# The step-size product of a state-space block: weights stationary in four column tiles, tokens moving

## The reference, cut to what matters

```python
xn = (x - mu) * jax.lax.rsqrt(var + EPS) * ln_w + ln_b
zxbcdt = xn @ in_proj_w.T                       # 512 tokens, 256 features -> 1288
z, xBC, dt = jnp.split(zxbcdt, [D_INNER, D_INNER + CONV_DIM], axis=-1)   # dt: 8 heads
dt = jax.nn.softplus(dt + dt_bias)
A = -jnp.exp(A_log)
def step(h, inputs):
    dtk, xk, Bk, Ck = inputs
    decay = jnp.exp(dtk * A)
    h = h * decay[:, :, None, None] + dtk[:, :, None, None] * xk[..., None] * Bk[:, None, None, :]
    y = jnp.einsum('bhpn,bn->bhp', h, Ck)
    return (h, y)
```

## Time and profile before

| | us |
|---|---|
| median of 3 runs | 1272.43 |
| the runs | 1271.83, 1272.43, 1276.07 |
| the profiled execution | 1279.79 |
| its span in the trace | 1278.0 |
| PE busy in the span | 1155.5 (90%) |
| PEld busy | 804.7 (63%) |
| DVE busy | 996.8 (78%) |
| ACT busy | 779.9 (61%) |
| POOL busy | 636.8 (50%) |
| mean granted clock of PE | 0.962 of full |

### The profile page before, as it was taken

The page is one execution under the profiler, slowest core; times in us unless marked ns, Lnnn a source line. Parts: engine busy times, 40 slices in busy tenths (PEclk is TensorE's granted clock), DMA queues, the critical chain, the costliest instruction groups (busy, mean ns, idle before and its releaser), DMA issues. The chain is left out here.

```text
span 1278.0 us, 29867 instructions
## 1 busy us (share of the span) xinstructions
PE 1155.5 (90%) x10284; PEld 804.7 (63%) x10284; DVE 996.8 (78%) x2529; ACT 779.9 (61%) x1444; POOL 636.8 (50%) x554
## 2 busy tenths in 40 slices
PE   4687999999999999999999999999999999877387
PEld 2255666676667677666767667767776676655244
DVE  5765788788878887788888887888888887754486
ACT  1224676667776577667666766767566776766242
POOL 4572376327832584446643774178244653300375
PEclk9798999999999999999999999999899999988699
DMA  6042105310432024401540052203240133110511
GB/s 205 0 116 75 51 1 145 114 34 26 120 91 81 26 67 101 120 6 34 142 126 17 26 149 76 67 26 104 75 120 5 52 87 104 31 46 15 206 74 61
DMA packets 101524, 96.52 MB, mean 76 GB/s; under 512 B 17184, under 2 KB 76832, under 8 KB 100096
## 3 DMA queue, kind: packets, MB, share of 16 engines
q1 hardware_dynamic: 92912, 76.42, 20.0%
q0 software_dynamic: 6240, 17.57, 5.8%
q10 hardware_dynamic: 2224, 0.62, 0.2%
HBM read 71.49 MB, written 27.26 MB: 77 GB/s over the span
## 5 line engine op out<-in xcount | busy, mean ns | idle before, releaser
L891 ACT ACTIVATE T<-T,nmx 128x512 f32<-128x512 f32 x512 | 368.8, 724 | 229.0 <-DVE nmx L1257 227.0
L1257 DVE CUSTOM_DVE_ANT_0 T<-ps,am 128x512 f32<-128x512 f32 x512 | 346.2, 684 | 124.7 <-PE ps L680 123.1
L688 PE MATMUL pt<-ident,T 128*128 128x128 f32 x2048 | 329.1, 285 | 13.6 <-ACT PT L882 12.9
L688 PEld LDWEIGHTS pt<-ident,T 128*128 128x128 f32 x2048 | 234.4, 144 | 120.7 <-issue 88.9
L882 ACT COPY PT<-pt 128x512 f32<-128x512 f32 x352 | 202.0, 574 | 15.9 <-PE pt L688 15.2
L1373 POOL TENSOR_TENSOR dmask<-triu,dA 128x1024 fp32r<-128x1024 f32 x64 | 132.6, 2137 | 49.6 <-DVE dA L1101 49.5
L680 PE MATMUL ps<-k_st,q_st 64*128 64x512 f32 x512 | 132.0, 510 | 26.4 <-DMA q_st<-q_d 25.9
L705 PE MATMUL po<-PT,va 128*32 128x128 f32 x4096 | 140.0, 278 | 10.5 <-issue 6.2
L705 PEld LDWEIGHTS po<-PT,va 128*32 128x32 f32 x4096 | 105.9, 110 | 33.6 <-issue 32.3
L1411 POOL TENSOR_TENSOR rr<-se,nhalf 128x1 f32<-128x1 f32 x32 | 22.2, 694 | 210.1 <-DVE se L1187 199.5
L1348 POOL TENSOR_TENSOR xc<-xc,ygT 128x512 f32<-128x512 f32 x90 | 119.7, 1330 | 13.4
(11 more groups left out here) (212 smaller groups left out, 1970.7 us busy)
## 6 DMA issues: line engine op xcount, KB each, us to landing
k_st<-k_d SPq DMA_DIRECT2D x256, 64.0 KB, 2.2
q_st<-q_d SPq DMA_DIRECT2D x256, 64.0 KB, 2.4
am<-in_mask SPq DMA_DIRECT2D x8, 1024.0 KB, 5.5
k_d<-kp SPq DMA_DIRECT2D x32, 256.0 KB, 2.6
am<-in_adj POOLq DMA_DIRECT2D x8, 1024.0 KB, 10.8
q_d<-qp SPq DMA_DIRECT2D x128, 64.0 KB, 1.6
x_in<-in_x SPq DMA_DIRECT2D x8, 512.0 KB, 4.5
ctx_in<-in_ctxT SPq DMA_DIRECT2D x8, 512.0 KB, 4.2
```

Of the source, the lines that this page charges most:

```text
L688: ins = pe.transpose(pt[u % 2][:, kt * P:(kt + 1) * P], T[:, u % RING, kt * P:(kt + 1) * P], ident[:, :])
L891: act.activation(T[:, u % RING, :], T[:, u % RING, :], ACT.Exp, bias=nmx[:, u % RING:u % RING + 1], scale=-1.0).then_inc(sems["probs"], 1)
L1257: dve.tensor_tensor_reduce(T[:, u % RING, :], ps[(a * UNITS + u) % S_BANKS][:, :], ams[a % 2][:, qt, :], -1.0, 3e38, ALU.add, ALU.min, nmx ...
```

## The change

The product is turned round. The weights become the stationary operand, padded with zeros from 8 to 32 columns, and the tokens move, 128 at a time: chunk c goes to column tile c, and the result lies with its heads on partitions 32c to 32c + 7 and the chunk's 128 tokens along the columns. ACT copies this tile to a part of `th` that is free then, PE turns it by one 128x128 transpose into a second PSUM tile, and DVE adds the bias as before, reading 8 of each 32 columns. DVE zeroes the padding once at the start.

```diff
-    ("lnT",): {"pe": -1000, "act": -990}, ("dt1",): {"pe": -955, "act": -960, "dve": -935}, ("bc", 4): {"pe": -915, "act": -915},
+    ("lnT",): {"pe": -1000, "act": -990}, ("dt1",): {"pe": -965, "act": -950, "dve": -935}, ("dtT",): {"pe": -950, "act": -965}, ("bc", 4): {"pe": -915, "act": -915},
...
-                "lnT": [("lnT", 0), ("lnT", 1)], "dt1": [("dt",)], "bc": [_s], "cum": [("cum",)], "z": [_s],
+                "lnT": [("lnT", 0), ("lnT", 1)], "dt1": [("dtT",)], "dtT": [("dt",)], "bc": [_s], "cum": [("cum",)], "z": [_s],
...
-        wdt = sb("wdt", [P, KE, NH])
+        wdt = sb("wdt", [P, KE, P // C])
...
                     if k == "dt1":
-                        pe.wait_ge(read(("dt",), b), free_at(("dt",), b))
+                        if b == 0:
+                            pe.wait_ge(setup["pad"], 1)
+                        pe.wait_ge(read(("dtT",), b), free_at(("dtT",), b))
                         for kt in range(KE):
                             pe.wait_ge(read(("lnT", kt), b), read_at(("lnT", kt), b))
-                        for c in range(C):
-                            for kt in range(KE):
-                                ins = mm(bank(("dt",), b)[:, c * NH:(c + 1) * NH], xnT[:, kt, c * P:(c + 1) * P], wdt[:, kt, :], kt == 0, kt == KE - 1)
-                        ins.then_inc(full(("dt",), b), 1)
+                        for kt in range(KE):
+                            for c in range(C):
+                                ins = pe.matmul(bank(("dtT",), b)[P // C * c:P // C * (c + 1), 0:P], wdt[:, kt, :], xnT[:, kt, c * P:(c + 1) * P],
+                                                start=(kt == 0), stop=(kt == KE - 1), tile_position=(0, P // C * c), skip_group_check=True)
+                        ins.then_inc(full(("dtT",), b), 1)
+                    if k == "dtT":
+                        pe.wait_ge(read(("dt",), b), free_at(("dt",), b))
+                        pe.wait_ge(read(("dtT",), b), read_at(("dtT",), b))
+                        pe.transpose(bank(("dt",), b)[:, 0:P], th[:, 0, 0:P], ident[:, :]).then_inc(full(("dt",), b), 1)
...
+                    if k == "dtT":
+                        act.wait_ge(sems["silu"], at("silu", b, 0))
+                        act.wait_ge(full(("dtT",), b), full_at(("dtT",), b))
+                        act.copy(th[:, 0, 0:P], bank(("dtT",), b)[:, 0:P]).then_inc(read(("dtT",), b), 1)
...
+                dve.memset(wdt[:, :, NH:], 0.0).then_inc(setup["pad"], 1)
...
-                        dve.tensor_tensor(dts[:, 0, :, :], bank(("dt",), b)[:, 0:C * NH].rearrange("p (c h) -> p c h", h=NH), dtb[:, :, :], ALU.add).then_inc(read(("dt",), b), 1)
+                        dve.tensor_tensor(dts[:, 0, :, :], bank(("dt",), b)[:, 0:P].rearrange("p (c h) -> p c h", c=C)[:, :, 0:NH], dtb[:, :, :], ALU.add).then_inc(read(("dt",), b), 1)
```

More of the change, by code:

```diff
@@ L114 @@
     ("ln1",): {"dve": -1905, "pool": -1795}, ("ln2",): {"dve": -1895}, ("ln2r",): {"dve": -1840, "pool": -1685, "sp": -1505},
-    ("lnT",): {"pe": -1765, "act": -1920}, ("dt1",): {"pe": -1635, "act": -1881, "dve": -1738}, ("bc", 4): {"pe": -1685, "act": -1898},
+    ("lnT",): {"pe": -1765, "act": -1920}, ("dt1",): {"pe": -1635, "act": -1881, "dve": -1738}, ("dtT",): {"pe": -1630, "act": -1885}, ("bc", 4): {"pe": -1685, "act": -1898},
     ("conv", 4): {"pool": -1654}, ("bc", 5): {"pe": -1555, "act": -1878}, ("conv", 5): {"dve": -1674}, ("bc", 0): {"pe": -1465, "act": -1793},
@@ L301, in build @@
         m_read = [sem(f"m_read{k}") for k in range(M_BANKS)]
-        setup = {n: sem(f"setup_{n}") for n in ("act", "dve", "pool", "scaled")}
+        setup = {n: sem(f"setup_{n}") for n in ("act", "dve", "pool", "scaled", "pad")}
         PER = dict(
@@ L369, in build @@
                     ((cw[:, :, :], t["conv_w"].rearrange("(k p) j -> p k j", p=P)), consts), (column(cb, "conv_b"), consts)]
-        act_loads = [(column(lnw, "ln_w"), ln_in), (column(lnb, "ln_b"), ln_in), (matrix(wdt, "wdt"), w_in), (row(alog[:, :], "A_log"), consts)] + [
+        act_loads = [(column(lnw, "ln_w"), ln_in), (column(lnb, "ln_b"), ln_in), ((wdt[:, :, 0:NH], t["wdt"].rearrange("(k p) n -> p k n", p=P)), w_in), (row(alog[:, :], "A_log"), consts)] + [
             (row(dtb[:, c, :], "dt_bias"), consts) for c in range(C)] + [((triu[:, :], t["triu"]), consts), (matrix(wk, "wk"), kv_in), (matrix(wv, "wv"), kv_in)]
```

## The result

The changed kernel takes **1268.35 us** (1265.79 to 1271.05, 10 runs); the kernel before, measured beside it, 1274.14 (1270.13 to 1278.18, 10 runs). The ratio is 0.9946, 95% interval 0.9927 to 0.9966: faster by 0.5%, more than the 0.3% that can be told from no change. The profiled execution took 1269.45 us, its span is 1267.7, its mean granted clock 0.969 (before 0.962).

A forecast was written before the change was run, and what follows sets the result against it. PE was taken to set the pace on average (97% busy), with DVE close behind at the change. From the median, 1272.43 + 0.3 (delay) - 2.5 (batch 1) - 1.0 (clock) = 1269.2 us; range 1263.5 to 1275.5.

The forecast's parts named there:

- likeliest case: Whole kernel: DVE late next, gain from batch 1 and the clock; 1269.2 us, spanning 1265 to 1273, chance 0.45.
- The product, 1.70 to 0.54, and the transpose, 0.12: Step-size product on PE: column tiles cut it from 1.70 to 0.54 us, turning transpose adds 0.12; PE saves 1.04 a batch.
- rival 4: Product on PE: column tiles go one behind the other, scores 1.7 us late in six batches; about 1278 us, chance 0.03.
- The copy on ACT, 0.3 and hidden: ACT before the exponential: the 128x128 copy takes 0.3 us (0.2 to 0.4), hidden in 2.99 us of idle time.
- What is late next is DVE; nothing of 1.04 us reaches the end: Batches 2 to 7: later scores delay DVE, PE waits some 0.9 us for the gate; +0.05 us a batch, +0.3 for six.
- Rival 2: Batches 2 to 7: saved PE time counts in full, next scores 0.9 to 1.04 us earlier; near 1263.5 us, chance 0.17.
- rival 3: Scores behind the product: their delay is passed on through maximum and gate, up to +4.0 us; 1276.4 us, chance 0.12.
- Batch 1, -2.5: Batch 1: product moves into PE's wait for the query DMA and a clock fall goes; -2.5 us, between 0 and -3.3.
- The clock in batches 2 to 7, -6.2 for the profiled execution, -1.0 for the median: Behind the products: without 8-column matmuls no fall to half clock; -6.2 us profiled (bounds 0 and -6.2), -1.0 for the median.
- the other runs probably met few: Runs other than the profiled one: few clock falls, so the median counts one smaller fall less part of it, -1.0 us.
- Rival 1: Behind the products: the clock falls as before, with transposes and a new 0.9 us wait; 1271.9 us, chance 0.23.
- the rule on transposes: Between the score pairs: transposes don't count as PE activity, so falls continue; the sum loses -1.0 and batch 1's 1.7 us.

The follow-up runs named there:

- the padded kernels: Old product's moving operand zero-padded from 8 to 64 columns, against the kernel before: 1271.78 us, ratio 0.9964, at its old place; 1275.31 us, 0.9986, moved ahead of the scores.
- the two repeats: The changed kernel run again unaltered, against the kernel before: 1270.39 us, ratio 0.9963, and 1270.58 us, ratio 0.9949.

## Why the prediction was right, and where it was not

The forecast, 1269.2 in a range of 1263.5 to 1275.5, held the 1268.35 measured, and its likeliest case is the one that happened. That the time was met to 0.9 us is luck in part: the gain was 5.8 us where 3.2 were foretold, and the forecast started from a median 1.7 us under that of the ten runs. By its own steps:

- **The product, 1.70 to 0.54, and the transpose, 0.12.** Measured 0.57 and 0.11. The four column tiles run beside each other (their first four instructions start within 0.02 us); rival 4 falls.
- **The copy on ACT, 0.3 and hidden.** 0.27 us, in 2.22 us of idle time; the turning transpose follows the first four transposes without a gap. Right.
- **What is late next is DVE; nothing of 1.04 us reaches the end.** Right: the scores come 0.57 later (0.54 foretold), PE waits 0.78 for the gate (0.9), and the bias addition is the last link. Rival 2 falls: its mark was a distance shorter by 0.5. The term itself, +0.05 us a batch, was mis-sized: it is +0.20 (5.67 to 5.87, and A to C in batches 3 to 7). The forecast's own working had the next scores 0.09 later; measured, the bias addition ends 0.42 later and not 0.36, and the scores follow its end by 0.48 us and not 0.44. The margin that counts is not the gate's 0.67 us of lead: the gate ends 0.42 later, and the transposes of yg start earlier than before. It is that of the bias addition, which had 0.40 us to the transposes of xnr and needs 0.14. The table shows one figure for three sizes of delay: B later by 0.57, 1.00 and 1.78 gives C later by 0.19, 0.62 and 1.40. Each time 0.38 is absorbed, and the rest stays to M. A part of the delay is passed on, then, as rival 3 had it, but by the bias addition and not by the gate; with a product of 0.57 us it costs 1.2 us in six batches and not 4.0, and with the old form, padded, 8 us (1275.31 against 1267.22).
- **Batch 1, -2.5.** The move alone measured -2.9, between -0.5 and -5.5 (-2.5 by the means, -1.6 by the medians). The cover was as described. Whether the move is what takes the clock's fall away there is open. Behind the scores the fall was there in 3 of 3 profiled executions, one of them with the padded form. With the thin form moved it came in one (batch 1 moved alone) and not in the other (all batches moved); with a padded or new form moved it came in 0 of 9.
- **The clock in batches 2 to 7, -6.2 for the profiled execution, -1.0 for the median.** The mechanism was right, as the padded kernels show. The size for the median was mis-sized, by the step "the other runs probably met few". Half of the time at half clock behind these products is 6.8, 5.1 and 3.4 us in the three profiled executions with the old form at its place, so the two executions beside that of the forecast met falls of 5.1 and 3.4. Padding alone gave 0.36%, 4.6 us, between 2.3 and 6.8, though the mean clock of its runs does not show it. Three runs of the kernel before had been too few to tell, with a median of 1272.43 where the later comparisons gave 1274.15 to 1276.73. Falls elsewhere, as that at 780.02, come and go in both kernels.
- **Rival 1 and the rule on transposes.** After the change, transposes stand between the scores with a wait of 0.78 us, and the clock is full in all these windows: behind 42 of 42 products of the new form, 24 of them with that wait, and behind 6 of 6 of the padded product with 0.89 us of wait. The Trainium skill ("TensorE: Matmul & The Clock Gate", part 4 on the PE-mode transpose) holds that transposes don't count as PE activity in the same way. That may be so, but it does not decide here: with the transposes kept and only the product's columns widened, the falls went. The Trainium skill ("TensorE: Matmul & The Clock Gate", part 1, "What's actually happening") has the clock follow how busy PE has been lately. The profile's busy time, which counts PE as busy with an instruction anywhere in it, does not agree with that here: in the repeat of the kernel before the clock fell behind a product through which PE was busy without a gap (1.66 of 1.66 us), and in the changed kernel it stays full where PE is busy for 3.67 of 4.54 us. A full record of busy time did not keep the clock.

Put together from the parts: +1.2 for the delay, -2.9 for batch 1, -4.6 for the clock, -6.3 us; measured -5.8 by the medians of the first comparison (-5.2 and -6.2 in the two repeats). The last two parts have some 2 us of scatter each, so that they add up is no proof. By another way: over the three later comparisons the kernel before has a mean time of 1275.96 us and a mean granted clock of 0.9664 (89 runs), the changed kernel, with the first comparison, 1269.94 and 0.9698 (34 runs). Span times clock is 1231.4 and 1229.8: of 6.0 us, 1.6 (give or take 0.7) are shorter work and waits, the rest is clock, wherever in the run it was lost.

## What to carry to other kernels

Ask of a short operation not only what it costs but what it is ahead of: moved ahead of the scores, a product that had shrunk by 1.0 us on PE made its batch 0.20 us longer, and behind them 0.22 shorter. Where the granted clock drops to half behind a block of matmuls with few moving columns, pad or swap the operands, and test that part alone; here padding, with batch 1's product moved, gave the whole gain. Look for the last thing that a delayed engine frees, and not only for the longest wait: PE waited 0.78 us for the gate, and it was the short bias addition behind it that set the next scores. Where a clock that comes and goes scatters the totals by 0.25%, take the price of a local edit from the starts of instructions and from span times clock, and the price of the clock from many runs.

## What was not expected of the hardware

- A matmul with 64 moving columns takes PE hardly longer than one with 8: a block of 16 from 817.65 to the scores at 819.48 (1.83 us) and from 817.40 to 819.28 (1.88).
- The same 16 thin matmuls between the same neighbours cost the clock one time in three at one place (6 of 18, three executions) and five times in six when moved by one pair of scores (one execution); moved, the fall began up to 4.2 us behind the start of the product, where in the old place it came 1.3 to 2.0 us behind.
- The distances between instructions around the product repeat to 0.05 us from run to run while the totals of one kernel scatter over 10 us and more. Much of that is the clock, and not all: in the first comparison's ten runs of the changed kernel span times mean granted clock stays within 1227.8 and 1231.0 while the times go from 1265.79 to 1271.05, but over the 89 runs of the kernel before it goes from 1226.9 to 1237.2, with times from 1268.66 to 1284.75.
